# First stage of a three-stage image kernel rebuilt: PE writes PSUM in step order, both norms share a round, and eight copies of each rstd row go through DRAM

## The reference

```
x = x + conv3x3_depthwise(ln_c(x))            # ln_c: norm over the 64 channels, eps 1e-6
t = tokens(x)                                 # (2, 65536, 64)
Wx = ln_t(t) @ W.T                            # ln_t: norm over channels, eps 1e-5
Wx = batchnorm(Wx) * gamma + beta             # mean and variance of each column over all tokens
y_t = sigmoid(Wx_t + y_{t-1} @ V.T)           # recurrence over the 65536 tokens
t = t + y
x = x + linear_attention(ln_c(x)); t = t + routed_ffn(ln_t(t))     # later stages
```

## Time and profile before

| | |
|---|---|
| median of 3 runs | 1888.73 us (1888.72 to 1892.98) |
| profiled execution | 1891.77 us, span 1890.0 us |
| first stage | about 20 us to 757 us of the span |
| batch norm's small phase | 759 us to 766 us |
| in 100 us to 600 us: PE, POOL, DVE, ACT busy | 99.8%, 94.3%, 91.3%, 76.1% |

### The profile page before, as it was taken

One profiled execution on the slowest core, in us unless ns is written; L12 is line 12 of the kernel. 1 busy time (PEld: TensorE's weight loads), 2 busy tenths in 40 slices (PEclk: granted clock), 3 DMA queues, 4 the chain that ended last, 5 costly groups with the idle time before them and its releaser, 6 DMA issues. The chain is left out here.

```text
span 1890.0 us, 24219 instructions
## 1 busy us (share of the span) xinstructions
PE 1537.0 (81%) x5627; PEld 635.5 (34%) x5627; DVE 1415.1 (75%) x2290; ACT 1236.0 (65%) x2177; POOL 1478.3 (78%) x1092
## 2 busy tenths in 40 slices
PE   3899999999999995499992769999999999825200
PEld 1333333333333331266651423333333333204200
DVE  1779999999998986499994547999999999961000
ACT  2777777777777762399992458889888898620000
POOL 2999999999999994048889129999999999911475
PEclk8999999999999997699997789999999999965555
DMA  4578888888878755859996527898888887652011
GB/s 153 165 219 250 251 254 239 249 245 250 254 235 257 229 173 177 334 216 421 424 405 269 214 48 220 282 293 287 284 272 282 289 290 245 205 163 48 1 2 2
DMA packets 111405, 429.80 MB, mean 227 GB/s; under 512 B 44672, under 2 KB 47648, under 8 KB 66208
## 3 DMA queue, kind: packets, MB, share of 16 engines
q1 hardware_dynamic: 91376, 423.77, 68.6%
q10 hardware_dynamic: 16432, 4.29, 1.4%
q0 software_dynamic: 3456, 0.19, 0.2%
HBM read 257.89 MB, written 170.01 MB: 226 GB/s over the span
## 5 line engine op out<-in xcount | busy, mean ns | idle before, releaser
L445 ACT ACTIVATE tap_products<-xn,kk 128x512 f32<-128x512 f32 x384 | 275.1, 718 | 165.7 <-POOL x_and_products L476 160.3
L476 POOL TENSOR_TENSOR x_and_products<-tap_products,x_and_products 128x512 f32<-128x512 f32 x256 | 327.0, 1277 | 41.7 <-POOL x_and_products L476 3.6
L376 PE MATMUL pst<-xn,taps 128*128 128x512 f32 x768 | 351.4, 593 | 0.0
L1462 POOL TENSOR_SCALAR exp_q<-exp_q 128x512 f32<-128x512 f32 x128 | 189.6, 1482 | 74.2 <-ACT exp_q L1413 74.2
L534 DVE SCALAR_TENSOR_TENSOR pst<-xn,kk,pst 128x512 f32<-128x512 f32 x256 | 192.1, 750 | 62.2 <-PE pst L376 62.0
L879 DVE SCALAR_TENSOR_TENSOR pss<-region,bn,pss 128x256 f32<-128x256 f32 x432 | 195.7, 489 | 45.8 <-PE pss L791 44.6
L376 PEld LDWEIGHTS pst<-xn,taps 128*128 128x128 f32 x768 | 145.4, 190 | 186.1 <-issue 186.1
L1457 POOL TENSOR_TENSOR sq_norm<-x_ring 128x512 f32<-128x512 f32 x128 | 188.6, 1473 | 5.4 <-DVE x_ring L1509 1.7
L476 POOL TENSOR_TENSOR x_and_products<-tap_products,x_ring 128x512 f32<-128x512 f32 x128 | 164.4, 1285 | 19.8 <-ACT tap_products L445 19.7
L828 POOL TENSOR_TENSOR x_block<-x_block,region 128x2048 f32<-128x2048 f32 x28 | 155.6, 5556 | 18.5 <-DMA x_block<-x_scratch 13.5
L416 ACT ACTIVATE sq<-x_ring 128x512 f32<-128x512 f32 x256 | 157.7, 622 | 16.2 <-POOL x_ring L483 10.1
(11 more groups left out here) (239 smaller groups left out, 2947.0 us busy)
## 6 DMA issues: line engine op xcount, KB each, us to landing
rstd_wide<-rstd_scratch SPq DMA_DIRECT2D x128, 512.0 KB, 7.1
x_ring<-in_x SPq DMA_DIRECT2D x32, 1024.0 KB, 5.3
x_scratch<-x_ring SPq DMA_DIRECT2D x32, 1024.0 KB, 4.3
xl_scratch<-wx SPq DMA_DIRECT2D x32, 1024.0 KB, 8.6
region<-xl_scratch SPq DMA_DIRECT2D x32, 1024.0 KB, 12.3
x_ring<-x_scratch SPq DMA_DIRECT2D x32, 1024.0 KB, 5.5
rstd_of_channels<-rstd_scratch SPq DMA_DIRECT2D x64, 512.0 KB, 7.6
out<-x_ring SPq DMA_DIRECT2D x32, 1024.0 KB, 6.6
```

Source lines behind the costliest of these rows:

```text
L376: m = pe.matmul(wide(pst[g % 2]), taps[:, n * P:(n + 1) * P], tap_rows(g, t), start=(n == 0), stop=(n == len(PE_TAPS) - 1))
L445: act.activation(prod[:, n, :, :], tap_rows(g, t), ACT.Copy, scale=kk[:, t:t + 1]).then_inc(products, 1)
L476: pool.tensor_tensor(xr[:, g % XR, :], prod[:, n, :, :].rearrange("p r w -> p (r w)"), xr[:, g % XR, :] if n else x_tile(g), ALU.add).then ...
L1462: pool.tensor_scalar(e, e, 1.0, None, ALU.min).then_inc(clipped, 1)
```

## The change

In the first stage, and in the small phase behind it:

- The taps are divided anew: PE has two, DVE four or five and ACT (with POOL's additions) three or two, for even and odd tiles.
- PE writes `psw` in step order (a stride of 128 bytes in PSUM from one column to the next), and likewise the statistics of the second norm, so its rstd rows come out in step order within a tile. DVE reads both contiguously and writes `u` in runs of 32 elements.
- Both norms share a round: 36 rounds in place of 64. The matrix `stat_of[l]` gives 8 equal rows to each norm and image in each quarter; the two norms are accumulated in one PSUM bank, so DVE subtracts, and ACT takes logarithm and exponential, once for both. The clamp moves from DVE to ACT. The second norm runs 16 steps behind in place of 14, and `SCALE`, `PROJECT` and `SQ1` move by 2.
- All 32 rows of a quarter go to DRAM, four DMAs of 32 x 512 a round; each image and norm then has 8 equal copies, 8 KB apart. A load of 64 partitions reads the 8 copies in turn, each 8 times.
- `bn_stats` and `bn_aggr` go. DVE's scaling gives the sum by its accumulator, ACT squares `u` and gives the sum of squares (`square_u`), and the small phase makes mean and variance from the two.

```diff
+            def taps_of(g):
+                return ((PE_TAPS[:2], [5, 6, 7, 8], [0, 1, 2]),
+                        (PE_TAPS[:2], [2, 5, 6, 7, 8], [0, 1]))[g % 2]
...
-            SQ, CENTER, TAPS, SUMS, FINISH, SQ1, PROJECT, SCALE = -4, 5, 8, 9, 10, 10, 18, 19
-            STATS = (0, 14)
+            SQ, CENTER, TAPS, SUMS, FINISH, SQ1, PROJECT, SCALE = -4, 5, 8, 9, 10, 12, 20, 21
+            STATS = (0, 16)
+            BEHIND = (STATS[1] - STATS[0]) // TPB
+            ROUNDS = NBLK + BEHIND
...
-                    for b in range(B):
-                        sp.dma_start(rstd_d[l][k, b, :].rearrange("(j n) -> j n", n=TILE),
-                                     rstd[16 * b:P:32, n % 2, :]).then_inc(rstd_out[n % 2], 16)
+                    for j in range(TPB):
+                        sp.dma_start(rstd_d[n, :, cols_of(j)],
+                                     rstd[32 * j:32 * j + 32, n % 2, :]).then_inc(rstd_out[n % 2], 16)
...
                     for b in range(B):
+                        copies = rstd_d[round_of(l, k), 16 * l + 8 * b:16 * l + 8 * b + 8, :]
                         sp.dma_start(rb[l][b * C:(b + 1) * C, k % 2, :],
-                                     rstd_d[l][k, b, :].partition_broadcast(C)).then_inc(rb_loaded[l][k % 2], 16)
+                                     copies.partition_broadcast(C // 8)).then_inc(rb_loaded[l][k % 2], 16)
...
-                    for j in range(TPB):
-                        m = pe.matmul(psm[32 * j:32 * j + 32, :], stat32[:, :], x_tile(TPB * k + j), start=True, stop=True)
+                    for l, k in norms:
+                        for j in range(TPB):
+                            x_in = in_chunks(x_tile(TPB * k + j))
+                            m = pe.matmul(by_norm(l, psm[32 * j:32 * j + 32, :]), stat_of[:, l, :], x_in,
+                                          start=(l, k) == norms[0], stop=(l, k) == norms[-1])
...
-                    pe.matmul(psw[g % 2][:, :], wcT[:, :], x_tile(g), start=True, stop=True).then_inc(wx_ready, 1)
+                    pe.matmul(by_step(psw[g % 2][:, :]), wcT[:, :], in_chunks(x_tile(g)), start=True,
+                              stop=True).then_inc(wx_ready, 1)
...
+                    act.activation(var[:, :], pse[:, :], ACT.Relu).then_inc(clamped, 1)
...
+                def square_u(g):
+                    act.wait_ge(u_ready, g + 1)
+                    if g:
+                        act.wait_ge(u_squared, g)
+                    act.activation(u_squares[:, :].rearrange("p (n c) -> p n c", n=CLEN), u_steps(g), ACT.Square,
+                                   accum_out=sums[:, 1, g:g + 1]).then_inc(u_squared, 1)
...
-                    dve.tensor_scalar(var[:, :], pse[:, :], 0.0, None, ALU.max).then_inc(clamped, 1)
...
-                    dve.tensor_tensor(by_chunk, psw[g % 2][:, :].rearrange("p (c n) -> p c n", n=CLEN),
-                                      rb[1][:, k % 2, cols_of(g % TPB)].rearrange("p (c n) -> p c n", n=CLEN),
-                                      ALU.mult).then_inc(u_ready, 1)
-
-                def statistics(g):
-                    dve.wait_ge(u_ready, TPB * (g // TPB + 1))
-                    dve.bn_stats(stats[:, g, :], u[:, g // TPB % 2, cols_of(g % TPB)]).then_inc(bn_done, 1)
+                    dve.scalar_tensor_tensor(out=u_steps(g), in0=stepped(psw[g % 2][:, :]), scalar=1.0,
+                                             in1=stepped(rb[1][:, k % 2, cols_of(g % TPB)]), op0=ALU.mult, op1=ALU.mult,
+                                             accum_out=sums[:, 0, g:g + 1]).then_inc(u_ready, 1)
...
-                dve.bn_aggr(bn[:, 0:2], stats[:, :, :].rearrange("p t n -> p (t n)")).then_inc(step, 1)
+                dve.tensor_reduce(bn[:, 0:2], sums[:, :, :], AX.X, ALU.add).then_inc(step, 1)
```

More of the change, by code:

```diff
@@ L64, in constants @@
     start = np.arange(P)[:, None] * N
-    return np.concatenate([eye, mean, eye - mean, heads, pair, base, iota] + later + [start], 1).astype(np.float32)
+    eps = np.where(np.arange(P)[:, None] % 32 < 16, EPS_C, EPS_T)
+    return np.concatenate([eye, mean, eye - mean, heads, pair, base, iota] + later + [start, eps], 1).astype(np.float32)
 def build_program(nc, x, conv_k, ffn_w, ffn_v, gamma, beta, q_w, q_b, kv_w, kv_b, proj_w, proj_b,
@@ L213, in build_program @@
             XR = 3
-            NP, ND = len(ACT_TAPS), len(DVE_TAPS)
+            NP = 3
+            def taps_of(g):
+                return ((PE_TAPS[:2], [5, 6, 7, 8], [0, 1, 2]),
+                        (PE_TAPS[:2], [2, 5, 6, 7, 8], [0, 1]))[g % 2]
+            dve_taps, act_taps = ([sum(len(taps_of(i)[who]) for i in range(g)) for g in range(NT + 1)] for who in (1, 2))
             X = sb("x_ring", [P, XSLOTS, BLOCK], F32, ph)
@@ L271, in block_at, with round_at @@
                 return k if rest == 0 and 0 <= k < NBLK else None
+            def round_at(t, lag):
+                n, rest = divmod(t - lag, TPB)
+                return n if rest == 0 and 0 <= n < ROUNDS else None
             def cols_of(s):
@@ L329, in _ @@
                 for t in range(-8, STEPS_A):
[L330 to L333, removed]
+                    if (n := round_at(t, 2)) is not None:
+                        rstd_to_dram(n)
+                    if (n := round_at(t, 3)) is not None:
+                        for l, k in norms_in(n):
                             rstd_to_channels(l, k)
@@ L489, in _ @@
                     if (g := tile_at(t, TAPS)) is not None:
-                        for n in range(NP):
+                        for n in range(len(taps_of(g)[2])):
                             add_product(g, n)
@@ L575, in _ @@
                         scale_wx(w)
-                    for l, k in rounds:
-                        variance(l, k)
                     if g is not None:
                         tap(g, 1)
-                    if (g2 := tile_at(t, SCALE + TPB)) is not None:
-                        statistics(g2)
-                    for l, k in rounds:
-                        clamp(l, k)
+                    if n is not None:
+                        variance(n)
                     if g is not None:
-                        tap(g, 2)
+                        for i in range(2, len(taps_of(g)[1])):
+                            tap(g, i)
                     if (g := tile_at(t, CENTER)) is not None:
@@ L618, in _ @@
                 pe.wait_ge(step, 1)
-                pe.matmul(bps[:, 0:1], pairm, bn[:, 0:1], start=True, stop=True).then_inc(mm, 1)
-                pe.wait_ge(step, 4)
-                pe.matmul(bps[:, 1:2], pairm, bn[:, 4:5], start=True, stop=True).then_inc(mm, 1)
+                pe.matmul(bps[:, 0:2], pairm, bn[:, 0:2], start=True, stop=True).then_inc(mm, 1)
             @blk.scalar
```

182 lines of the change are left out of this document (100 added, 82 removed).

## The result

The changed kernel takes 2123.2 us (median of 4 runs, 2115.4 to 2124.2), the one before 1889.5: a ratio of 1.122, with an interval of 1.119 to 1.125. The forecast was 1840, and the range ended at 1915. Its profiled execution took 2123.5 us.

The account below looks back on a forecast made before the run. POOL was taken to set the pace at 5.30 us a tile, PE 0.1 behind. At 4.95 a tile 127 tiles save 44.5 and the ends 3.5: 1891.8 less 48, less 3.0 for the median, rounded 1840 us; range 1812 to 1915.

Parts of the forecast that it names:

- the loads of the rstd rows: Second norm's last row reaches DVE's scaling at 20.6 us at worst, 17.0 at best: 5.0 or 4.1 us a tile.
- its slow form: Rival: rstd loads run on 8 of 16 engines at 14.9 GB/s each, 7.2 us a tile, near 2125 us; chance 8%.
- the full rate of 25.6: Rival: rstd loads on 8 engines at 25.6 GB/s each, 5.35 us a tile, 1892 us; chance 20%.
- the fast form: Rival of 8 engines at 25.6 GB/s each for rstd loads: 5.35 us a tile, 1892 us; chance 20%.
- PE's strided writes: Rival: matmuls writing PSUM with a 128-byte stride at double price, PE 5.69 us a tile, 1932 us; chance 12%.
- The compute: Engine sums per tile in the first stage: DVE 4.80 us, POOL 4.66, PE 4.37, ACT 4.2.
- Two taps with dependents: Part of DVE's tile: two taps that the next tap waits for cost 1.57 us, 0.785 each.
- DVE's sum: DVE's work in the first stage: 4.80 us a tile, 5.07 with the upper scaling, 4.50 if no dependence costs.
- its sum of 4.66: POOL's work in the first stage: 3.5 additions a tile at 1.33 us each.
- The first half of the loads' step: Loads follow the first store by 3.3 us; at 238 GB/s the last row lands at 20.6, 5.0 us a tile.
- The wait that I took the middle of: DVE's wait for rstd rows: middle of 4.80 and 5.0 us a tile, plus 0.05 for other waits, giving 4.95.
- The ends: First stage's ends: 5.9 us less in the batch norm's end, 2.4 more for filling and drain, net -3.5 us.

Follow-up runs that it names:

- before_8x8: The kernel before the change, with only the loads' source pattern written as 8 times 8 repeats of the same row in place of 64: 2096.3 us, ratio 1.110.
- four_by_16: The changed kernel with each load reading four of the eight copies, 16 repeats outermost: 1857.2 us, ratio 0.983.
- rows_16: The changed kernel with the eight copies stored twice (eight stores a round), loads with 16 rows outermost and 4 repeats inside: 1915.1 us, ratio 1.014.
- distinct_rows: The changed kernel with one-copy loads, each bringing 64 different rows of x in place of one row 64 times (output not valid): 1861.0 us, ratio 0.985.
- overlapping_rows: The changed kernel with one-copy loads, each bringing 64 rows 512 bytes apart in the rstd scratch (output not valid): 1863.5 us, ratio 0.986.
- after_late: The changed kernel with PROJECT and SCALE two steps later, loads still with 8 outermost: 2050.6 us, ratio 1.085.
- f16_late: The changed kernel with loads of four copies, 16 repeats outermost, and PROJECT and SCALE two steps later: 1808.0 us, ratio 0.957.
- one_row_late: The changed kernel with every row stored once and read 64 times, and PROJECT and SCALE two steps later: 1809.1 us, ratio 0.957.

## Why the prediction was wrong

**The step that failed** is the one on the loads of the rstd rows: "At 238 GB/s, what the engines moved while they were full with such loads, that is 4.4 us". The 238 belongs to a load whose outermost count is 64. The new one has 8 there, is carried by 8 engines, and goes at 106 to 119 GB/s. I had the right mechanism among the rivals, in its slow form ("If an engine keeps today's 238 / 16 = 14.9 GB/s ... T = 7.2, near 2125"), and gave it 8%. Measured: 111 / 8 = 13.9 GB/s for an engine, 7.24 us a tile in the steady stage, 2123 us. `before_8x8` shows it with nothing else changed, `four_by_16` and `rows_16` show that 16 outside undoes it.

That 2125 and 2123 agree so closely is in part luck: T over all tiles is 6.95, with which the same sum gives 1841 + 2.00 x 127 = 2095, and the ends, forecast at -3.5, brought 24.

The Trainium skill ("DMA: Bandwidth & Descriptors", Why a DMA increments its semaphore by 16 and not by 1) says that a DMA runs on the largest number of engines up to 16 that divides the outermost dimension of both sides. Every run here agrees: while only the loads are open, the DMA share is 0.48 to 0.52 with 8 outside, and full with 16 or 64.

**Why I gave it so little.** My reason was "eight engines ask for half the traffic of one row, and the rows are eight now". It took reading one row for the cause of the 238. `distinct_rows` and `overlapping_rows` show that it isn't: an engine moves 14 GB/s of such a load whatever rows it reads. The price of an engine then was in the earlier trace rows all along, and the full rate of 25.6, to which I gave 20%, was the price of another shape.

**Latency or bandwidth.** The rival was worked out as a chain of latencies, and its 7.2 is the steady pace of 7.24. As a rate it comes out close to that. A block has 2.1 MB of loads at 111 GB/s, 18.9 us on the eight engines. The other 3.4 MB (x in, x1 and u out, the small stores), if spread over all 16 at 410 / 16 GB/s each, are 8.3 us. Together 27.2 of the 29.0 us of a block, as an estimate. I take it that these eight engines carry their part of the plain blocks late, behind the loads. It fits a stretch in which the share is half and the rate 201 GB/s, 25 for each of eight:

```profile
414.00:416.00 2.00, 0.00 (x0) 0.00 (x0) 0.61 (x1) 0.00 (x0) 0.00 (x0) 0.50 0.50 201
```

The DMA share of the changed kernel in the 500 windows of 1 us from 100 to 600 us checks the sum. If the first half of a window's share is put down to the eight engines, they are idle for 34 of the 500 us, or 27.0 us busy in a block. The other eight come to 11 us, not 8.3: plain blocks beside the loads are slower than 25.6 GB/s an engine. So in the changed kernel the latency ends the block, and the eight engines have 2 us to spare. In `after_late` they are idle for 13 of the 500 us only. Its steady pace, (836.8 - 141.0) / 104 = 6.69, is 26.8 us a block, the estimate of 27.2 within 2%: there the rate sets the pace. "The eight engines would be busy 10.2 us with loads and 7.5 with their share of the rest, below 4T" held for the fast form alone. In `before_8x8` the same working gives 26.6 us for a block of 28.2.

**PE's strided writes**, the 12% rival, are false: 0.86 us apart as before, and in `f16_late` PE is busy 94% of the stage, as 4.37 us of a 4.65 us tile at the plain price would have it. (Its 1932 was a slip besides: 1841 + 0.74 x 127 = 1935.) The Trainium skill ("PSUM — Partial Sum Buffer", Specifications (TRN2)) says that any non-contiguous pattern slows matmuls significantly; for these float32 writes, one value every 128 bytes, the rows show no slowing.

**The compute.** In `f16_late` DVE is 98% busy, the 97% forecast. The scaling takes 414.25 - 413.65 = 0.60 from start to start against 0.72: its accumulator read (0.08) costs nothing, since the next instruction starts at the same 414.25. Two taps with dependents take 415.83 - 414.25 = 1.58, against 1.57. An even tile is 417.75 - 413.65 = 4.10 us (4.19 forecast), an odd one 413.65 - 408.75 = 4.90 (4.98). From one tile to the eighth behind it two scalings start 342.45 - 304.80 = 37.65 us apart:

```profile
304.80 0.69 DVE L615 SCALAR_TENSOR_TENSOR wx<-psw,rstd_wide 128x512 f32<-128x512 f32 x1
...
342.45 0.69 DVE L615 SCALAR_TENSOR_TENSOR wx<-psw,rstd_wide 128x512 f32<-128x512 f32 x1
```

That is 4.71 us a tile where DVE's sum was 4.80: 0.09 too dear, by the scaling. The mean of 4.65 is lower, since POOL's first 48 tiles go at (275.74 - 54.98) / 48 = 4.60 each, near its sum of 4.66. DVE's first scaling is at 111.8 us, so I take it that DVE is ahead until then and is caught up with later.

**The first half of the loads' step** held: loads follow the first store by 3.06 us in `four_by_16` (3.3 forecast; 423.51 - 419.43 = 4.08 in the changed kernel), and 238 GB/s gave "T = 5.0 us a tile", measured 5.01 and 5.05. Had the loads used 16 engines, the kernel would have come out at 1857, inside the range. The wait that I took the middle of was real, and `f16_late` removes it.

**The ends** were forecast at -3.5 us. The batch norm's end is shorter, but by less than the 5.9 worked out: from the last scaling to `wT` it is 998.66 - 990.60 = 8.1 us where it was 765.48 - 753.45 = 12.0. And the first addition starts 61.9 - 54.8 = 7.1 us later, and from the last addition to `wT` it is 998.7 - 944.6 = 54.1 us where it was 765.5 - 728.3 = 37.2: filling and draining wait for the slow loads too. With 16 engines, in `four_by_16`, the ends still cost 4.3 us more, not 3.5 less (0.6 less before the first addition, 4.9 more behind the last). The stage of the changed kernel is (6.95 - 5.30) x 127 + 7.1 + 16.9 = 233.6 us longer, and the span 2121.5 - 1890.0 = 231.5.

**What stays open** is why the 64-partition and the 16 x 8 loads run at half the rate of a plain block of 128 partitions on as many engines. Repeats, one row read by many and the size of the packets are excluded, and a second queue brought nothing. That the engines meet in one part of SBUF was only thought of, and no run tells it apart.

The best version found is `f16_late`, 1808.0 us, 4.3% below before. `one_row_late`, without any copy, is as fast within the measurement. So the rebuilt stage, with its loads on 16 engines and the later steps, is worth about 82 us, and the eight copies add nothing to it.

## What to carry to other kernels

Before a DMA's pattern is changed, read the outermost count of its source and destination: 8 there meant 8 of 16 engines and 205 us on this kernel, with no byte more. When a rate is taken from the trace, take it per engine and for the same shape of transfer, and see how full the engines that carry it will be, not the mean of all. A trick that spreads reads over copies needs a run that shows that reading one copy is slow.

## What was not expected of the hardware

After a long wait PE comes back slowly. Behind DVE's stall of 8.3 us, PE's timeline in the changed kernel has four tap matmuls:

```profile
418.94 3.75 PE L432 MATMUL pst<-xn,taps 128*128 128x512 f32 x4 [7.53 <-DVE acc L600]
```

And the table of stages, with the granted clock third from the end:

```profile
420.00:422.00 2.00, 2.00 (x4) 0.94 (x3) 1.97 (x5) 2.00 (x5) 1.86 (x3) 0.50 0.25 61
```

They last 3.75 us, the four at 404.38 lasted 1.88: the clock is at 0.50 (1.2 GHz) after PE had been idle for 7.5 us, and 0.84 in the mean of the stage, where it was 1.00. It does not fall at once: in the next block's stall the row of 441 to 443 us still shows 1.00. A stall thus costs more than its own length on PE, though here DVE waited only 5.2 us in ten times for PE's taps in 500 us.
